# A new table of nominal times, and so another program order on every engine, in a fused convolution, attention and expert kernel

## What is computed

```
x = x + conv3x3(sign(batchnorm(groupnorm(x))), sign(W) * scale)      # padding with +1
t = x as 3136 tokens of 32 channels per image
t = t + attention(layernorm(t))     # 16 heads, linear attention: q, k = elu(.) + 1,
                                    # cos/sin weights of the position, k^T v summed over the tokens,
                                    # q (k^T v) / (q sum(k)), dense layer
t = t + experts(layernorm(t))       # router softmax over 8 experts, best two, weighted sum
```

## Time and profile before

| what | value |
|---|---|
| device time, median of 3 runs | 2821.83 us (2802.16, 2821.83, 2821.90) |
| span of the profiled execution | 2819.6 us |
| its own device time | one of the two runs near 2822 us, some 2.2 us above its span |
| DVE, PE busy | 83%, 86% of the span |
| ACT, POOL busy | 61%, 66% |
| matmuls and other instructions | 19300 on PE, 3041 DVE, 2821 ACT, 1479 POOL |
| mean granted TensorE clock | 0.929 of full speed |

### The profile page before, as it was taken

How to read it: one execution, slowest core, us unless ns; L and a number is a source line. 1 busy time by engine, 2 the same in 40 slices (tenths; PEclk the granted TensorE clock), 3 DMA queues, 4 the chain that set the end, 5 groups by cost and what they waited for, 6 DMA issues and landing times.

```text
span 2819.6 us, 56945 instructions
## 1 busy us (share of the span) xinstructions
PE 2421.4 (86%) x19300; PEld 1207.1 (43%) x19300; DVE 2342.6 (83%) x3041; ACT 1724.8 (61%) x2821; POOL 1866.9 (66%) x1479
## 2 busy tenths in 40 slices
...
PEclk7579999999999999999999999999999999999995
...
DMA packets 232233, 55.14 MB, mean 20 GB/s; under 512 B 226065, under 2 KB 226945, under 8 KB 231777
## 3 DMA queue, kind: packets, MB, share of 16 engines
...
## 4 chain that ended last, share of the span: by engine, by line
PE 40%; DVE 22%; POOL 17%; issue 14%; ACT 3%; DMA 1%; SPq 1%; POOLq 0%; DVEq 0%; ACTq 0%
PE ps L585 10%; PE ps L576 5%; PE ps L610 5%; DVE kbuf L994 5%; POOL prod L844 5%; DVE qbuf L1000 5%; PE ps L627 4%; PE ps L636 3%; POOL prod L847 3%; DVE rs L1017 2%; DVE route L1064 2%; POOL rstd L793 2%; PE ps L601 2%; ACT ebuf L716 2%; PE ps L568 2%
## 5 line engine op out<-in xcount | busy, mean ns | idle before, releaser
L716 ACT ACTIVATE ebuf<-ps,small 112x1024 f32<-112x1024 f32 x448 | 498.6, 1113 | 384.7 <-PE ps L576 357.3
L994 DVE SCALAR_TENSOR_TENSOR kbuf<-ps,ebuf 112x1024 f32<-112x1024 f32 x448 | 546.8, 1221 | 129.4 <-ACT ebuf L716 112.0
L721 ACT ACTIVATE ebuf<-ps,small 128x896 f32<-128x896 f32 x448 | 450.1, 1005 | 317.7 <-PE ps L601 237.8
L815 POOL TENSOR_TENSOR qbuf<-spread_r,qbuf 128x896 f32<-128x896 f32 x224 | 468.2, 2090 | 141.0 <-ACT spread_r L751 140.8
L585 PE MATMUL ps<-kbuf,xcs 112*64 112x512 f32 x1792 | 506.3, 651 | 45.1 <-DVE kbuf L994 45.1
L1000 DVE SCALAR_TENSOR_TENSOR qbuf<-ps,ebuf 128x896 f32<-128x896 f32 x448 | 486.3, 1085 | 37.6 <-ACT ebuf L721 35.3
L793 POOL TENSOR_TENSOR rstd<-varr,power 112x28 f32<-112x28 f32 x64 | 307.2, 4801 | 292.7 <-DVE varr L984 290.7
L636 PE MATMUL ps<-qbuf,gmat 128*64 128x224 f32 x3584 | 403.2, 369 | 4.5 <-DVE pbuf L1028 1.7
L844 POOL TENSOR_TENSOR prod<-prod 112x512 f32<-112x512 f32 x224 | 285.3, 1274 | 159.0 <-DVE prod L1084 157.9
L1084 DVE TENSOR_TENSOR prod<-ps,gate 112x1024 f32<-112x1024 f32 x224 | 272.4, 1217 | 94.4 <-PE ps L661 79.9
L627 PE MATMUL ps<-rs,sel 128*128 128x448 f16 x896 | 249.4, 360 | 96.6 <-issue 81.7
...
## 6 DMA issues: line engine op xcount, KB each, us to landing
...
xt<-in_x SPq DMA_DIRECT2D x128, 98.0 KB
out<-ffn SPq DMA_DIRECT2D x128, 98.0 KB
shifted<-nat SPq DMA_DIRECT2D x128, 52.6 KB, 5.0
...
```

The costliest lines, as they stand in the source:

```text
L716: act.activation(ebuf[0:PT, 0, :].rearrange("p (a b) -> p a b", a=2), o[0:PT, :, :], ACT.Exp, bias=minus_one[0:PT, :]).then_inc(kexp_made, 1)
L721: act.activation(ebuf[:, 1, 0:2 * G * PT].rearrange("p (a b) -> p a b", a=2), o[:, :, 0:G * PT], ACT.Exp, bias=minus_one).then_inc(qexp_ma ...
L815: nc.gpsimd.tensor_tensor(qbuf[:, 2:4, n, :], spread_r[:, :, :], qbuf[:, 2:4, n, :], ALU.mult)\
L994: v.scalar_tensor_tensor(kbuf[:, n % 2, :].rearrange("p (a b) -> p a b", a=2), o[0:PT, :, :], 1.0, ebuf[0:PT, 0, :].rearrange("p (a b) -> ...
```

## The change

All nominal times in `schedule()` and all `SHIFTS` are others. No instruction, buffer or wait is added or taken away; the file is five lines shorter, so that line numbers after the table are smaller by five. Two lines of the table and the shifts of one engine, as a sample:

```diff
-    add("SM1", [-7.96])
+    add("SM1", [-11.44])
-    add("RP", [13.85, 14.97, 15.97, 17.79, 18.78, 21.48, 23.54])
+    add("RP", [13.08, 14.28, 14.98, 16.29, 17.59, 20.72, 21.54])
...
-    "gpsimd": {"F": -2.19, "RP": -1.61, "T2": -1.77},
+    "gpsimd": {"CS": 4.86, "F": -1.65, "GT": -3.87, "OUT": -4.07, "PL1": -3.05, "PL2": 2.96, "PN1": 3.49,
+               "PN2": 0.19, "RP": -2.36, "T2": -2.23},
```

More of the change, by code:

```diff
@@ L142, in add @@
         s.extend((t, kind, n) for n, t in enumerate(times))
-    add("XT", [-23.13, -22.48])
-    add("CV", [-13.11, -12.76])
-    add("XC", [-9.58])
-    add("SM1", [-7.96])
-    add("PN1", [-9.24])
-    add("XH1", [-6.50])
-    add("PL1", [-9.21])
-    add("CS", [-6.97, -6.70])
-    add("ZT", [-5.63, -1.39])
-    add("K", [-3.29, -2.86, -1.80, -0.32, 1.58, 1.92, 2.48, 3.24, 3.92, 4.87, 5.09, 5.90, 6.46, 6.99])
-    add("KX", [-2.14, -1.87, 0.27, 1.02, 1.92, 3.45, 3.85, 4.93, 5.21, 5.42, 5.94, 7.03, 7.90, 8.06])
@@ L157, in schedule @@
-    add("KT", [8.36])
-    add("G", [9.46, 9.86])
-    add("Q", [4.11, 4.96, 5.65, 6.06, 6.46, 7.66, 8.18, 9.13, 11.09, 11.34, 11.83, 13.42, 14.97, 15.59])
-    add("DN", [11.12, 11.19, 11.42, 11.50, 16.30, 16.54, 16.56, 16.68])
-    add("SU", [12.02, 17.39])
-    add("RC", [12.07, 17.64])
-    add("RL", [13.24, 18.20])
-    add("R", [14.96, 15.05, 15.84, 16.71, 19.33, 20.27, 24.24])
-    add("RP", [13.85, 14.97, 15.97, 17.79, 18.78, 21.48, 23.54])
-    add("NM", [15.85, 18.60, 20.07, 20.58, 22.99, 23.72, 26.77])
@@ L170, in schedule @@
-    add("TB", [15.28])
-    add("T2", [21.90, 24.63, 24.96, 27.84])
-    add("S2", [24.40, 27.26, 27.43, 29.55])
-    add("SM2", [29.73])
-    add("PN2", [27.61])
-    add("XH2", [31.86])
-    add("PL2", [30.69])
-    add("ZU", [33.29, 33.68])
-    add("LG", [34.09])
-    add("RT", [34.52, 34.80, 35.84, 36.19, 36.22, 36.95, 37.18])
-    add("GT", [35.17])
-    add("F", [37.89, 38.65, 39.01, 39.68, 40.71, 42.71, 44.87])
-    add("OUT", [46.76])
+    add("XT", [-24.14, -23.34])
+    add("PN1", [-17.31])
@@ new lines, in schedule @@
+    add("CS", [-14.79, -11.79])
+    add("CV", [-14.45, -13.54])
+    add("SM1", [-11.44])
+    add("XC", [-10.93])
+    add("XH1", [-8.16])
+    add("PL1", [-7.75])
+    add("ZT", [-6.30, -2.45])
+    add("K", [-4.38, -3.66, -2.55, -1.21, 0.54, 0.91, 1.06, 1.88, 2.79, 3.86, 3.98, 4.74, 5.56, 5.92])
+    add("KX", [-3.23, -1.67, -0.88, 0.05, 0.97, 2.10, 2.91, 3.87, 4.15, 4.57, 4.89, 6.46, 6.67, 7.34])
+    add("Q", [2.98, 3.91, 4.65, 4.95, 5.62, 6.62, 7.16, 8.31, 9.88, 10.38, 10.52, 12.26, 13.90, 14.65])
```

26 lines of the change are left out of this document (21 added, 5 removed), and 6 rows, old and new, of the table SHIFTS.

## The result

The changed kernel took 2710.5 us (median of 4 runs, 2709.0 to 2712.8), the kernel before 2816.9 in the same rounds (4 runs, 2802.2 to 2821.9). The profiled execution spans 2709.7 us, 109.9 less than before.

What follows compares the result with a forecast made beforehand. No single engine bounds it: PE's work plus idle time the order forces on PE. Terms 0.65 + 0.6 + 0.7 + 0.6 = 2.55, taken as 2.5 us over 26 images, 65 us: from 2822 to 2757 us, range 2715 to 2815.

Steps and rivals of the forecast that it cites:

- RP4, XT0 (and K9, ZU0): PE's stops there: RP4 0.5, XT0 0.9, K9 none; 1.4 us instead of 2.05, gain 0.65 us an image.
- Q7, G0, NM5, G1: PE's stops around the choice of experts: 1.9 us instead of 2.49, gain 0.6 us an image.
- RP0: PE's stop there, with KX1 behind Q11: 0.6 us instead of 1.28, gain 0.7 us an image.
- jump: PE's stop where the loop jumps back, once every two images: still 3.25 us at its new place.
- the clock's term: Half-rate matmuls behind PE's stops cost about 2.4 us an image; shorter stops return a quarter, 0.6, ends 0 and 1.5.
- every long stop is followed by matmuls that take longer: On PE, from one image: KX7 1.95 us against KX8's 1.08, NM5 2.71 against NM4's 1.69, KX2 1.98.
- I go by the row: At Q7: trusts the profile row with line 1064 at 3.33 us, not the port rule by which Q7 waits for nothing.
- rival A: Line 1064 on DVE slips between CS0's two POOL instructions, Q6 ready early: 4 us an image, 2718 us, chance 0.17.
- Cover of 9 and 15 us: cost nothing: On POOL, PN1 ahead of RP4 and OUT: these end later but well before they are wanted, so no cost.
- the rest: SP, jump, R5, K11 and others: shift and load DMAs have most of an image of slack, jump cost unchanged.
- B: POOL reaches T21 1.5 to 2 us late, ACT stops before K1's exponential; only 0.65 left: 2805 us, chance 0.15.
- C: POOL's products RP5 and RP6 each hold up one more instruction of the choice of experts: slower, 2854 us, chance 0.08.

Runs made afterwards that it cites:

- the first run: Kernel before with only the moves around Q7, G0, F0 and the gates: 2875.7 us, ratio 1.019.
- the last combined variant: Kernel before with all the change's loop moves except DN4, KX3 and S23; jump, SP order and prologue numbers as before: 2734.4 us.

## Why the prediction was wrong

The direction was right, and so was the place of most stops: nothing is added, and PE waits less. The size was 65 us for 110. The terms of the sum, us an image, with what they measured:

| term | forecast gain | measured |
|---|---|---|
| RP4, XT0 (and K9, ZU0) | 0.65 | 0.02 |
| Q7, G0, NM5, G1 | 0.6 | 1.21 |
| RP0 | 0.7 | 0.39 |
| jump | 0 | 0.15 |
| all idle time of PE in the loop | 1.95 | 1.24 |
| clock (busy time of PE in the loop) | 0.6 | 2.15 |

The stops of the first four rows shrank by 1.77 us; small new ones, such as Q11's 0.23, take half a microsecond back. So the stops gained less than forecast, and the step that failed is the clock's term. Over 26 images it makes 40 us of the miss of 45; the stops make -18, and what lies outside the loop 22.

- **"I take a quarter of the 2.4 us back, 0.6", the clock's term.** It measured 2.15 us an image, beyond the end of 1.5 that I gave it. I had taken the loss as proportional to the stops. It is not: with the stops of 1.5 and 2.3 us cut to 0.3 to 1.1, KX7 and NM5 came to their full rate wholly, and the mean granted clock of the loop went from 0.95 to 0.99. The 2.4 us were also read from one image. NM5 was slow in about every second image only, so "every long stop is followed by matmuls that take longer" does not hold for the others. KX7's 0.87 and NM5's 0.6 on average are some 1.5 of the 2.15; the rest is in other rows, and no run takes it apart.
- **"I go by the row", the step that kept line 1064 at 3.33 us.** This failed too, and it is where the clock's gain at NM5 comes from. The line took 0.46 us on average in the loop and Q7 waited for nothing instead of 1.4 us. With that rival A's outcome came about at this line, though not between the two halves of CS0: the instruction began under the second half and went in while POOL waited for ACT's copy. I had seen that RP5 overtakes a waiting DVE instruction, and left it at that; the question was whether POOL would be idle between CS0 and RP5 in the new order, and my walk was not fine enough to tell 0.3 us. With K11 moved back or added, the hold and 51 and 57 us went together. NM5 at 1.05 instead of 0.1 is the hold that moved to RT4 beside RP6: with RP6 moved back it is gone.
- **The moves costed at nothing.** "Cover of 9 and 15 us: cost nothing" for PN1 asked only who waits for RP4 and OUT. It missed that OUT would otherwise run beside SM1's small instruction and hold it. The PN1 move gains 41 us. K11, under "the rest", goes with the 51 to 57 us of line 1064.
- **Nothing taken for the other images.** The loop's 26 images give 26 x 3.38 = 88 us; 22 us are prologue, tail and the rest (10.7 us before the first TB, 3.9 behind the last).

Near their forecasts were RP4 (0.5, measured 0.34), XT0 (0.9, 0.91) and the jump (3.25 a pass, 2.9). But ZU0's stop of 0.83, for its bank of K9, was not foreseen and takes back the whole 0.65 of that place. RP0 was 0.89 for 0.6; 0.2 of it are S20 and S21 in front of K1, as the variants with and without them show (0.67 and 0.89). RP6 in front of the gates is not hidden, since it holds RT4 and so makes the stop of NM5; behind F0 it costs 13 us more in the one run of that. Of the rivals, B was there in small: "ACT idle in front of S21 for POOL" was named as its sign, and ACT waits 0.79 us there. C's hold of two products in front of Q6 came in the first run, not in the changed kernel. The walk over PE before speaks of seven stops; its rows and its sum have six.

The Trainium skill (SBUF — State Buffer, Who interferes with whom) says that a VectorE instruction with two SBUF inputs and a GpSimd instruction that reads SBUF exclude each other for a whole instruction. In the forecast I weighed it against the row of before and took the row. Both hold at once: line 1064 does wait for a whole POOL instruction, and for RP5 behind it too where that follows without a gap (3.33 us); it goes in where POOL stands idle for 0.2 to 0.3 us (0.43), and in front of T20 even without a gap.

What stays open: why the loop is so regular (in the changed kernel, from the second row of TB on, an image without the jump takes 76.03 to 76.07 us every time, and one with it 80.5 to 81.2), why RP5 goes in front of a waiting DVE instruction and T20 does not, what the 24 us between the last combined variant and the changed kernel are made of, and how the clock chooses at a stop of 2 us. The kernels of one run (2713.2, 2723.3, 2723.5, 2734.4, 2738.8, 2751.7, 2761.9, 2773.6, 2810.3) have no interval; kernels with four runs spread by 4 to 18 us. So +13 for RP6 is not sure, and neither is a difference of 3 us.
